# Causal attention of the last layer: probabilities transposed in 32x32 blocks on VectorE, products with the values on 32-row tiles

## The reference

```
def _attention(x, wq, wk, wv, wo):              # x: 4 x 512 x 128
    q = (x @ wq).reshape(b, t, 16, 64)          # 16 query heads of 64
    k = (x @ wk).reshape(b, t, 4, 64)           # 4 key and value heads
    v = (x @ wv).reshape(b, t, 4, 64)
    q = q * cos + _neg_half(q) * sin            # rotary
    k = k * cos + _neg_half(k) * sin
    scores = einsum('btghk,bThk->bghtT', q, k)
    scores = where(tril, scores, -inf) / sqrt(64)
    p = softmax(scores, axis=-1)
    out = einsum('bghtT,bThv->btghv', p, v)
    return out @ wo                             # 1024 x 128
h = x + _attention(_rmsnorm(x, g1), wq, wk, wv, wo)
```

## Time and profile before

| | us |
|---|---|
| median of 3 runs | 1642.51 |
| lowest, highest | 1641.46, 1645.33 |
| the profiled execution | 1644.7 |
| its span in the trace | 1642.9 |
| PE busy in it | 1404.0 |
| DVE busy | 954.7 |
| ACT busy | 759.9 |
| POOL busy | 240.2 |

### The profile page before, as it was taken

One profiled execution on the slowest core, in us unless ns is written; L12 is line 12 of the kernel. 1 busy time (PEld: TensorE's weight loads), 2 busy tenths in 40 slices (PEclk: granted clock), 3 DMA queues, 4 the chain that ended last, 5 costly groups with the idle time before them and its releaser, 6 DMA issues.

```text
span 1642.9 us, 43728 instructions
## 1 busy us (share of the span) xinstructions
PE 1404.0 (85%) x17627; PEld 873.3 (53%) x17639; DVE 954.7 (58%) x2511; ACT 759.9 (46%) x1942; POOL 240.2 (15%) x219
## 2 busy tenths in 40 slices
PE   5888888696499999999958999898989998899855
PEld 3343443393267666766643467445644565346545
DVE  4364644323477776877733676656764776567632
ACT  1313132251266665766622277225734474337534
POOL 3011210123030030110001200021001200030035
PEclk9989999798699999999978999898998999999968
DMA  9600000023230100100022000000000000000021
GB/s 330 234 17 1 18 1 7 17 61 97 77 144 4 25 21 10 36 4 17 4 57 68 1 2 1 5 13 2 2 5 11 4 1 1 1 14 2 2 89 52
DMA packets 57655, 59.72 MB, mean 36 GB/s; under 512 B 27869, under 2 KB 43104, under 8 KB 56304
## 3 DMA queue, kind: packets, MB, share of 16 engines
q1 hardware_dynamic: 54640, 51.63, 10.0%
q0 software_dynamic: 2528, 5.27, 1.0%
q10 hardware_dynamic: 288, 0.03, 0.0%
HBM read 33.22 MB, written 24.14 MB: 35 GB/s over the span
## 4 chain that ended last, share of the span: by engine, by line
PE 72%; DVE 14%; issue 4%; ACT 3%; DMA 2%; SPq 2%; POOL 2%; ACTq 0%; POOLq 0%; DVEq 0%
PE ps L1136 7%; PE ps L1524 6%; PE ps L1543 5%; PE ps L259 5%; PE ps L505 5%; PE ps L1557 4%; PE ps L1116 4%; PE ps L1126 4%; DVE arena L592 4%; PE ps L1157 4%; PE ps L1512 3%; PE ps L479 3%; PE ps L1171 2%; PE ps L1566 2%; PE ps L807 2%
## 5 line engine op out<-in xcount | busy, mean ns | idle before, releaser
L1269 DVE TENSOR_REDUCE nmax<-ps 128x1 f32<-128x512 f32 x256 | 166.7, 683 | 57.9 <-PE ps L1126 57.3
L1599 ACT ACTIVATE arena<-ps,arena 128x512 f32<-128x512 f32 (+3 forms) x256 | 135.3, 531 | 117.4 <-DVE arena L1662 109.1
L1662 DVE TENSOR_REDUCE arena<-ps 128x1 f32<-128x512 f32 (+3 forms) x256 | 124.3, 487 | 76.5 <-PE ps L1528 74.8
L1229 ACT ACTIVATE arena<-ps,nmax 128x512 f32<-128x512 f32 x172 | 119.0, 692 | 82.4 <-DVE nmax L1269 81.2
L1543 PE MATMUL ps<-sqc,arena 128*128 128x128 f32 x640 | 108.6, 292 | 20.0 <-DVE arena L1670 19.8
L1277 DVE COPY arena<-ps 128x512 f32<-128x512 f32 x128 | 88.0, 687 | 37.8 <-PE ps L1136 36.2
L592 DVE TENSOR_REDUCE arena<-ps 128x8 f32<-128x1232 f32 x64 | 88.9, 1437 | 30.1 <-PE ps L467 30.1
L1670 DVE TENSOR_SCALAR arena<-arena 128x512 f32<-128x512 f32 (+3 forms) x256 | 100.8, 394 | 9.1
L259 PE MATMUL ps<-identb 128*128 128x512 bf16 x366 | 104.8, 450 | 1.4 <-DVE kcol L713 1.4
L1524 PE MATMUL ps<-arena 64*128 64x384 f32 (+3 forms) x512 | 106.0, 493 | 0.0
L604 DVE RECIPROCAL arena<-ps 128x128 f32<-128x128 f32 x8 | 7.7, 958 | 160.7 <-PE ps L505 160.7
(11 more groups left out here) (357 smaller groups left out, 2658.9 us busy)
## 6 DMA issues: line engine op xcount, KB each, us to landing
xs_d<-onehot SPq DMA_DIRECT2D x4, 2560.0 KB, 23.9
cw<-in_cw SPq DMA_DIRECT2D x2, 2048.0 KB, 13.0
rv<-in_rv SPq DMA_DIRECT2D x2, 1536.0 KB, 19.4
late<-in_gw SPq DMA_DIRECT2D x3, 1024.0 KB, 10.9
arena<-gs_d SPq DMA_DIRECT2D x23, 129.0 KB, 2.1
onehot<-q_s SPq DMA_DIRECT2D x96, 8.0 KB
arena<-xs_d SPq DMA_DIRECT2D x23, 64.0 KB, 1.8
xs_d<-arena SPq DMA_DIRECT2D x23, 64.0 KB, 1.6
```

Of the source, the lines that this page charges most:

```text
L1229: nc.scalar.activation(PB[k % 6], ps[:, k % 5, :], ACT.Exp, bias=nmax[:, u:u + 1], accum_out=rsum[:, b % 2, u:u + 1]).then_inc(SD["exp"], 1)
L1269: nc.vector.tensor_reduce(nmax[:, k % NU:k % NU + 1], ps[:, k % 5, :], AX.X, ALU.max, negate=True)\
L1599: nc.scalar.activation(TF["p%d" % (n % 2)][:, h * S:h * S + wd], ps[:, FSB[n % 2][h], 0:wd], ACT.Exp, bias=TF["nmax"][:, k4:k4 + 1], accum ...
L1662: nc.vector.tensor_reduce(TF["nmax"][:, k4:k4 + 1], ps[:, FSB[n % 2][h], 0:wd], AX.X, ALU.max, negate=True)\
```

## The change

Only stage F changes, and one bank number in stage G.

1. `flip` moves from PE to DVE. `nc.vector.transpose` transposes each 32x32 block where it lies: the partitions stay in four groups of 32 queries, and in group g, block column k, stand the 32 keys of block k as rows and the 32 queries of group g as columns. It goes from SBUF to SBUF, so `copy` is gone.
2. `norm` moves from DVE to ACT (`ACT.Copy` with the reciprocal as scale, in place); the reciprocal stays on DVE, one for both heads (`invert`).
3. `values` now has only 32 keys on the partitions of one product. For each head pair it runs over 16 key blocks k, with 2 heads x 4 query groups = 8 products of 32 rows and 64 columns of weights, each on its own tile of the array, each streaming the queries of its group in all tiles i that see the block: 128, 96, 64 or 32 columns. The three parts are blocks 0 to 4, 5 to 9 and 10 to 15; they stand behind scores(n + 2) for n = 4m + 2, 4m + 3 and 4m + 4, two head pairs later. Behind the scores of 256 columns stands none.
4. Each of the four query groups needs all values on its own partitions: `sp_F` sends 16 DMAs of 32 partitions x 4 KB (2 MB) per batch from SBUF to SBUF, after ACT's copy of v. The first `flip` waits for them (it also overwrites v).
5. All eight `project` stand at the end of the batch, seven in a row ahead of the last `values`; they accumulate in bank 0, since banks 4 to 7 now take `values`.
6. `scores(n)` waits for exp of unit n - 2 itself, which the wait of flip had implied. Buffers move (probabilities have one tile per width; keys in `onehot` and `dec_row`; later query tiles in `rv`; the warming matmuls of stage G write bank 6).

The core of the diff:

```diff
@@ pe_F
-            def flip(n):
-                ...
-                for h in range(2):
-                    pe.wait_ge(SF["nrm"], b * 2 * NUF + 2 * n + h + 1)
-                    for j in range(i + 1):
-                        ins = nc.tensor.transpose(ps[:, FTB[h], j * P:(j + 1) * P],
-                                                  TF["p%d" % (n % 2)][:, h * S + j * P:h * S + (j + 1) * P], c["ident"])
...
+            def values(a, lo, hi):
+                if lo == 0:
+                    pe.wait_ge(SF["t"], b * 2 * NUF + 2 * NT * (a + 1))
...
+                for k in range(lo, hi):
+                    t = k // 4
+                    v0 = t * VW + (2 * a) % HKV * KD
+                    for h in range(2):
+                        for g in range(4):
+                            rows = slice(GR * g, GR * (g + 1))
+                            m = PTF[a % 2][h][rows, t * (S - P) + k * 32:t * (S - P) + k * 32 + 1]
+                            ins = nc.tensor.matmul(ps[HALVES[h], 4 + g, t * 32:P], V4[k % 4][rows, v0 + h * KD:v0 + (h + 1) * KD],
+                                                   bass.AP(m.tensor, m.offset, [list(m.ap[0]), [S - P, NT - t], [1, 32]]),
+                                                   start=(k == 0), stop=(k == 4 * NT - 1), skip_group_check=True,
+                                                   tile_position=(GR * g, KD * h))
...
             for n in range(NUF):
-                a, r = n // NT, n % NT
-                flip(n)
                 if n + 2 < NUF:
                     scores(n + 2)
-                if n >= 1:
-                    values(n - 1)
-                if r == 2 and a >= 1:
-                    project(a - 1)
-            values(NUF - 1)
+                if n > NT + 1 and n % NT != 1:
+                    values((n - 2) // NT - 1, *((0, 5), (5, 10), (10, 4 * NT))[(n - 2) % NT])
+            values(NTQ - 2, 10, 4 * NT)
+            pe.wait_ge(SF["exp"], (b + 1) * 2 * NUF - 2)
+            for a in range(NTQ - 1):
+                project(a)
+            values(NTQ - 1, 0, 4 * NT)
             project(NTQ - 1)
@@ act_F
+                nc.scalar.activation(p, p, ACT.Copy, scale=TF["rinv"][:, k4:k4 + 1]).then_inc(SF["nrm"], 1)
...
             for n in range(NUF):
                 if n + 1 < NUF:
+                    exp(n + 1, 0)
                     exp(n + 1, 1)
-                copy(n, 0)
-                copy(n, 1)
-                if n % NT == 0 and n:
-                    gather(n // NT - 1)
-                if n + 2 < NUF:
-                    exp(n + 2, 0)
+                if n % NT == 1 and n > 2 * NT:
+                    gather(n // NT - 2)
+                norm(n, 0)
+                norm(n, 1)
@@ dve_F
+                nc.vector.transpose(PTF[a % 2][h][:, i * (S - P):i * (S - P) + wd], TF["p%d" % i][:, h * wd:(h + 1) * wd])\
+                    .then_inc(SF["t"], 1)
...
             for n in range(NUF):
-                if n + 1 < NUF:
-                    norm(n + 1, 0)
+                if n:
+                    flip(n - 1, 0)
+                    flip(n - 1, 1)
                 if n + 2 < NUF:
                     top(n + 2, 0)
+                    top(n + 2, 1)
                 if n + 1 < NUF:
-                    norm(n + 1, 1)
-                if n + 2 < NUF:
-                    top(n + 2, 1)
+                    invert(n + 1)
@@ new
+        def sp_F(sp, b):
+            sp.wait_ge(SF["v"], b + 1)
+            for g in range(4):
+                for k in range(4):
+                    sp.dma_start(V4[k][GR * g:GR * (g + 1), :], TF["v"][GR * k:GR * (k + 1), :]).then_inc(SF["vd"], 16)
```

More of the change, by code:

```diff
@@ L1520, in scores @@
                     pe.wait_ge(SF["qm"], b * 2 * NTQ + 2 * (4 + n) + 2)
+                else:
+                    pe.wait_ge(SF["exp"], b * 2 * NUF + 2 * (n - 2) + 2)
                 if n % NT == 0:
@@ L1631, in act_F @@
+                norm(n, 1)
+            gather(NTQ - 2)
             gather(NTQ - 1)
```

133 lines of the change are left out of this document (67 added, 66 removed).

## The result

| | before | after |
|---|---|---|
| median of 16 runs (us) | 1644.90 | 1651.35 |
| lowest, highest | 1641.35, 1651.03 | 1641.03, 1662.58 |
| the profiled execution | 1644.7 | 1651.33 |
| its span | 1642.9 | 1649.5 |

The ratio of after to before is 1.0037, with a 95% interval of 1.0020 to 1.0054: slower by 0.4%, where 28.5 us or 1.7% faster was forecast. The time lies inside the range of 1582 to 1655, near its upper end, and on the other side of no change. The sum was short by 37 us.

A forecast was written before the change was run, and what follows sets the result against it. PE bounds stage F's stretches before; afterwards ACT was to, at 8.0 us per period against 10.3. Four stretches of 81.5 us, 326.0 against 354.5, save 28.5 from 1644.7: 1616.2, less 2.2 for the median, 1614; range 1582 to 1655.

The forecast's parts named there:

- The sum: Four main stretches of stage F at 81.5 us each, 326.0 against 354.5: 28.5 us less, giving 1614 us.
- transfers: Copies of v to the query groups in stage F: hidden before the first `flip`, with 2.7 us to spare at worst.
- the price of `values`: PE in stage F: 3.0 to 4.1 us per period, 3.8 taken; upper bound 3.5 before part starts, at 13.8 ns per record.
- The third: PE in `values` cannot issue narrow products fast enough: 1644 us at 0.31 a block (chance 0.04), 1692 at 0.40 (0.03).
- its mild case: PE in `values` at 0.31 us a block, 19 ns a record: 89 us per stretch, 1644 us; chance 0.04.
- the fifth: Stage F unchanged: late values, or the loop of score and exp, takes the gain of 7 us per stretch; chance 0.03.
- The first: `norm` on ACT costs only the copy it replaces, 2.5 instead of 3.4 us per period: 1586 us; chance 0.15.
- The second: Block transpose on DVE needs two cycles per element; DVE bounds at 9.7 us per period: 1660 us; chance 0.12.
- The fourth: Clock drops in the steady part of stage F, adding 6.2 us per affected period; 1680 us with a third; chance 0.05.

The follow-up runs named there:

- the wide run: Changed kernel with `values` in the earlier kernel's product form (128 partitions, 20 products per head pair, not 128; output not the attention's): 1600.14 us, ratio 0.9728 to the kernel before.

## Why the prediction was wrong, step by step

Most of its steps were right. With the products in the wide form, the plan of the change did what the sum said: 79.4 us per stretch, for 81.5 forecast, and 1600 for 1614.

| step | forecast | measured |
|---|---|---|
| block transpose of 512 columns | about 0.7 us | 0.688 |
| `norm` of 512 | 0.69, 0.58 apart | 0.732, 0.61 apart |
| period, from the fourth on | 8.0 | 8.7 mean (8.1 to 9.7); 8.1 with the wide products |
| third period, the first with `values` | 8.0 | 9.3 to 10.3; 8.8 to 9.4 wide; 8.1 with half the products |
| part 1 of `values`, full clock | 1.2 to 1.5 | 1.37 |
| `values` of one head pair in the tail | 3.5 | 8.0 (1014.36 to 1022.39) and 5.1 (from 1031.38) |
| seven projections | 6.6 | 9.0 in batches 0 and 3 at a mean clock of 0.70; 6.45 in batch 2 at 1.00 |
| last exp behind first scores | 64.2 | 69.4 mean; 66.0 wide |
| from there to the end | 17.3 | 20.6; 13.4 wide |
| clock early in a batch | 0.50 for 10 to 14 us | 0.67 mean of the first 21 us, so 14 us of it at 0.50 |
| clock in the tail | not in the sum | 0.50 again behind the stops, for 6.8, 3.4 and 6.8 us in batches 0, 2 and 3 |
| transfers | hidden | no wait of the first `flip` |

**The step that failed** is the price of `values`: "upper bound, if 13.8 ns per record is the fastest there is". As a rate within a burst it about held: in rows without a stop, at clock 1.00, a record starts 15 ns after the one before at 128 columns, 13 at 96, and 11 at 64 and 32, 3.2 us for a head pair. It was no upper bound, because it was read from 64 records in a row, less than one packet, and such a row cannot show what a supply by packets does to several hundred. A term was missing beside the work of the three engines, the supply of instructions: the 288 records of a period are 2.25 packets, at 3.3 to 3.9 us each 7.4 to 8.8 us. And in the tail, 256 records in a row took 8.0 us for the 3.5 of the sum. Of the 10.6 us by which a stretch of the changed kernel is longer than the wide run's (90.05 against 79.4), 3.4 come up to the last exp and 7.2 behind it. Of these 7.2, the stops by issue are 4.0, and the projections at the lower clock 1.3; the rest goes with the wide products, which are themselves shorter (2.7 us for 3.85), so not all of the 10.6 is supply.

**The rivals.** The third, that PE cannot issue the narrow products fast enough, had the place right and a chance of 0.07, and its mild case, 1644, lies nearest among the times that rivals name; the fifth, no change, is about as near. Its mechanism, a price for each record, is not what was found: a burst runs at full speed until the packet is used up, and half the records had no stop at all. The first was wrong: `norm` takes 732 ns, more than the exp. The second was wrong: the block transpose takes 280 ns for 128 columns and 688 for 512, 1.06 ns a column, the slope of `top`. The Trainium skill says one element per cycle and lane in "Vector Engine (DVE) Microarchitecture Reference", section "3.8 The reshape front-end and per-opcode configuration", and the trace agrees. The fourth came true for no period in the middle: from the fourth period to the last exp the mean clock was 1.00 in all four batches. The Trainium skill's least distance of 25 ns between matmuls ("TensorE: Matmul & The Clock Gate", section "Wait — 56ns, not 53.3ns?") does not hold on eight tiles: 80 records in 1.37 us are 17 ns each, with the part's start and drain in it, and 11 to 15 within a row. The fifth, late values, is there as a consequence: DVE waits 22 us for them.

**What could have been read beforehand.** The page of before has 17627 records and 142 packets on PE's instruction queue, 124 to a packet. With that division the change needed 6284 / 124, 51 packets more, all in stretches of 32 periods. The pace was in the same trace as well: in the stages between 400 and 850 us packets stand as close as 3.4 us, and 25 distances are under 4.3.

**What stays open.** Why 2.2 us and more pass from the start of a packet to the end of a stop, when the packet's own transfer record lasts about 1 us, and why the next does not start earlier. That a stop ends with the arrival of a packet is read from the times of all stops and from the count of 128, not shown by taking the queue away. And the cause of the wider scatter of the changed kernel's runs, 21.6 us for 9.7, was not tried.

## What to carry to other kernels

Count instructions as a resource of PE beside its columns: divide the matmul records of each stretch by 128, multiply by 3.5 us (this kernel had 3.3 to 3.9), and compare with the length of the stretch; a rate read from a short burst says nothing of it. Where many small products cannot be avoided, put work with few instructions between them (here projections: 20 us for a change of order alone, part of it by the clock). And when a step moves to another engine, ask of the cheapest-looking replacement not only how long it runs but how many instructions it is made of.

## What the runs showed of the hardware

- PE's instructions come in packets of 16 KB for 128 records with their weight loads, in every run, and never closer than 3.2 us (3.3 in the changed kernel). A burst of narrow products uses one up in 1.9. When PE runs dry it goes on 2.2 to 2.9 us after the start of the next packet, always 128 records or a multiple behind the last such stop.
- In a profile this looks like idle time by "issue" amid a row of products: 37 us of them here.
- Products on 32-row tiles and on the whole array taking turns cost more than rows of each: 1.13 us for 12 small and 2 wide records at a clock of 0.50, where the same records in rows of one kind take about half of that at the same clock (17 ns a small, 124 to 163 a wide record). At clock 1.00 such rows take 11.6 ns a small and 68 to 90 ns a wide record.
- Scaling on ACT from SBUF with a pointer takes 732 ns for 512 columns, more than exp with its row sum from PSUM, 689.
